# Starting the mixture of experts inside cross attention, with the token weights moved into the up product

## The chip, the cores and the metric

One core of one Trainium2 chip runs the whole program. The metric is the device time of one execution in microseconds. TensorE (PE, with its weight loads shown apart as PEld), VectorE (DVE), ScalarE (ACT), GpSimd (POOL) and SyncE (SP, which only issues DMAs here) each run an instruction queue in order and wait for each other by semaphores.

## What is computed

A decoder block on 16 batches of 56 tokens with 128 features, in float32:

```python
x = x + self_attn(layernorm(x))                  # token and channel diffusion
x = x + cross_attn(layernorm(x), ctx)            # ctx: 16 x 1500 x 128, 16 heads of depth 8
x = x + moe(layernorm(x))
# moe: E, I, K = 8, 512, 2
logits = x_flat @ gate_w.T                       # 896 tokens x 8 experts
top_v, top_i = top_k(logits, 2); probs = softmax(top_v)
combine = sum of probs * one_hot(top_i)          # weight of each token for each expert
for each expert e:
    hidden = silu(x_flat @ wg[e].T) * (x_flat @ wu[e].T)
    out += combine[e][:, None] * (hidden @ wd[e].T)
```

Every expert is computed for every token; the weight is zero for six of the eight.

## The kernel before

The kernel has three stages. The first is self attention. The second is cross attention, one batch after another in a software pipeline (`pipelined`, bodies for batch 0, a loop over pairs, and the last three batches unrolled). A batch has 12 slots `t`, one for each 125 keys: in each TensorE makes the scores (L1307), ScalarE their exponentials (L1103), and at slots 0, 5 and 9 TensorE weighs values (L1323) for four slots at once. Score banks are used in turn, so scores of slot t wait for the exponential of t-2. Between them the projections and maxima of the next batches are placed. At slot 8 the output projection of the batch before stands (L1339), and VectorE adds it to `X` (L1195). `X` holds two batches (a pair) side by side, 56 rows from partition 0 and 56 from partition 64, eight pairs.

After the last weighing come the denominators (L1332), their inverse (L1185), the output product and the residual of batch 15. Then the block ends: all engines meet, and a second block holds the experts. There VectorE takes the statistics of all eight pairs (L128, L133), GpSimd the power -1/2 (L156, L159), VectorE normalises (L138), TensorE transposes (L1646), ScalarE copies the transposed tokens twice, once rounded (`T_hi`) and once in full (`T3`, L1533), and VectorE subtracts them (`T_lo`, L1560). SyncE moves `X` by 23 small DMAs into `X3`, 7 tiles of 128 tokens without gaps.

A matmul on rounded operands (fp32r) takes one pass; a plain float32 one appears as two instructions. Gate and up products are therefore split: hi x hi, hi x lo, lo x hi, three passes of 448 columns (half of the tokens), where the weights are rounded by ScalarE (L1525) and their remainder is taken by GpSimd (L1506). An expert has 8 units: 2 halves of tokens x 4 tiles of 128 hidden features. In each unit TensorE makes gate (L1684 to L1686, banks 0 and 1) and up (the same lines, banks 2 and 3), ScalarE the SiLU (L1541), VectorE the product with up (`hidden`, L1629). The down products of the expert before stand between the units, plain float32, with the hidden tile as the still operand and `w_down` moving, four t of 128 x 128 for each of the 7 token tiles (L1664). VectorE multiplies each tile's result by the tokens' weight and adds it to `X3` (L1618). The routing (L1569 to L1604) runs on VectorE between the first expert's products; its exponential (L1545) stands on ScalarE between SiLUs. The result leaves in one DMA (L1497). Weights are loaded with two buffers; the first two experts' loads stand on SP behind cross attention's last batch.

The two calls of the units' order are, on TensorE:

```python
for side, done in ((0, gate_done), (1, up_done)): ...three passes...      # L1680
if later(e, 1) and k < TT:
    down(e - 1, 1 - j, k)                                                # L1688
```

## Time and profile before

| | us |
|---|---|
| median of 3 runs | 646.02 (645.42 to 651.07) |
| profiled execution, whole | 653.12 |
| its span, first to last instruction | 651.3 |
| cross attention's last weighing ends, in the span | 496.39 |
| first gate product starts | 515.55 |
| last down product ends | 647.52 |

In the rows that follow, a time is microseconds from the span's start. Shapes are partitions x elements, "x448" is the number of instructions. "Busy" of a group is the time in which at least one of them runs: matmuls overlap, so the mean duration of one is longer than the distance from one to the next. The granted clock of TensorE is given as a share of 2.4 GHz; 0.50 is 1.2 GHz.

### The profile page before, as it was taken

The page shows a single profiled execution, that of the slowest core. Times are in us where ns is not written, and L with a number is a line of the kernel's source. Part 1 is how long each engine was busy: PE and PEld are TensorE (multiplying, and loading weights), DVE is VectorE, ACT ScalarE, POOL GpSimd, SP SyncE. Part 2 cuts the span into 40 slices and gives each one's busy share as a digit, 9 for nine tenths or more (in the row PEclk, how much of TensorE's full clock was granted, in tenths as well). Part 3 has the DMA queues.
Part 4 walks back from the last instruction along what each step waited for, and adds up shares of the span by engine and source line. Part 5 has one row for each costly group of instructions (what it writes and reads, how often), then busy time and mean ns, then how long its engine had stood idle before and what let it go on. Part 6 is the DMA issues. An engine that isn't in the chain of part 4 may idle for free. (4 is left out here: it accounts for less than half of the span.)

```text
span 651.3 us, 17561 instructions
## 1 busy us (share of the span) xinstructions
PE 593.1 (91%) x6732; PEld 481.7 (74%) x6732; DVE 427.2 (66%) x799; ACT 338.2 (52%) x506; POOL 183.2 (28%) x149
## 2 busy tenths in 40 slices
PE   3799787798999999999999999999985699999997
PEld 1566374376877877877877787787774589999997
DVE  4765357866887788778788788877822464444443
ACT  2466445274666576567566566657564353333321
POOL 4685305622223323224223232322100221111100
PEclk9789789798999999999999999999998599999999
DMA  5000006498267356446536736734620011111100
GB/s 211 1 3 3 0 3 133 94 193 192 68 132 183 96 140 144 119 117 142 144 92 141 172 88 127 179 100 91 144 100 1 17 46 49 48 48 48 48 17 29
DMA packets 26190, 60.29 MB, mean 93 GB/s; under 512 B 14368, under 2 KB 15392, under 8 KB 26152
## 3 DMA queue, kind: packets, MB, share of 16 engines
q1 hardware_dynamic: 26152, 59.77, 38.3%
q8 instruction: 26, 0.43, 0.3%
q14 instruction: 12, 0.10, 0.0%
HBM read 20.48 MB, written 0.46 MB: 32 GB/s over the span
## 5 line engine op out<-in xcount | busy, mean ns | idle before, releaser
L1163 DVE TENSOR_REDUCE chunk_max<-PS 128x1 f32<-128x500 f32 x336 | 214.3, 673 | 62.2 <-PE PS L1283 60.5
L1103 ACT ACTIVATE P<-PS 125x896 f32<-125x896 f32 x192 | 173.3, 913 | 124.1 <-PE PS L1307 123.4
L1283 PE MATMUL PS<-k_hi,q_block_hi 128*128 128x500 f32 x336 | 131.3, 438 | 6.5 <-ACT k_full L246 3.3
L1307 PE MATMUL PS<-q_stack,k_stack 97*125 97x224 f32 x768 | 122.5, 283 | 4.3 <-DMA q_stack<-neg_rows 2.4
L1307 PEld LDWEIGHTS PS<-q_stack,k_stack 97*125 97x125 f32 x768 | 106.9, 190 | 19.3 <-issue 8.9
L255 POOL TENSOR_TENSOR k_lo<-k_full,k_hi 128x500 fp32r<-128x500 f32 x48 | 61.1, 1276 | 104.7 <-ACT k_full L246 102.4
L1283 PEld LDWEIGHTS PS<-k_hi,q_block_hi 128*128 128x128 f32 x336 | 60.9, 193 | 37.1 <-ACT k_full L246 16.7
L1629 DVE TENSOR_TENSOR hidden<-gated,PS 128x448 f32<-128x448 f32 x64 | 39.6, 619 | 69.2 <-PE PS L1686 63.8
L1323 PE MATMUL PS<-P,values 125*32 125x112 f32 x3072 | 84.4, 262 | 0.6 <-ACT P L1103 0.5
L1323 PEld LDWEIGHTS PS<-P,values 125*32 125x32 f32 x3072 | 72.6, 110 | 14.3 <-issue 10.8
L1541 ACT ACTIVATE gated<-PS 128x448 f32<-128x448 f32 x64 | 34.8, 544 | 80.5 <-PE PS L1686 76.0
L1036 POOL TENSOR_TENSOR q_stack<-q_copies,consts 96x896 fp32r<-96x896 f32 x16 | 26.8, 1677 | 132.1 <-PE PS L1307 131.6
L1664 PEld LDWEIGHTS PS<-w_down,hidden 128*128 128x128 f32 x448 | 57.6, 191 | 1.5
L1664 PE MATMUL PS<-w_down,hidden 128*128 128x128 f32 x448 | 57.9, 274 | 0.0
L217 PE MATMUL PS<-ctxT,mats 128*128 128x500 f32 x96 | 50.2, 607 | 4.3 <-ACT k_full L246 2.7
L1684 PE MATMUL PS<-T_hi,w_hi 128*128 128x448 f32 x128 | 52.2, 408 | 1.5 <-DVE hidden L1629 1.5
L225 PE MATMUL PS<-mats,ctxT 128*125 128x128 f32 x384 | 49.9, 273 | 0.0
L225 PEld LDWEIGHTS PS<-mats,ctxT 128*125 128x125 f32 x384 | 48.0, 188 | 1.4 <-issue 0.2
L1686 PE MATMUL PS<-T_hi,w_lo 128*128 128x448 f32 x128 | 47.4, 371 | 0.0
L1685 PE MATMUL PS<-T_lo,w_hi 128*128 128x448 f32 x128 | 47.3, 370 | 0.0
L245 ACT ACTIVATE k_hi<-PS,cols 128x500 fp32r<-128x500 f32 x48 | 32.2, 670 | 24.1 <-PE PS L217 23.4
L1506 POOL TENSOR_TENSOR w_lo<-w_gate_up,w_hi 128x1024 fp32r<-128x1024 f32 x8 | 19.0, 2380 | 91.1 <-ACT w_hi L1525 91.1
(153 smaller groups left out, 666.7 us busy)
## 6 DMA issues: line engine op xcount, KB each, us to landing
k_stack<-k_hi SPq DMA_DIRECT2D x128, 187.5 KB, 4.5
ctxT<-ctx_in SPq DMA_DIRECT2D x16, 750.0 KB, 4.3
k_stack<-k_lo SPq DMA_DIRECT2D x64, 187.5 KB, 4.4
w_gate_up<-wgu_in SPq DMA_DIRECT2D x8, 512.0 KB, 3.7
w_down<-wd_in SPq DMA_DIRECT2D x8, 256.0 KB, 2.7
q_stack<-neg_rows SPq DMA_DIRECT2D x112, 0.5 KB
mats<-mats_in SPq DMA_DIRECT2D x1, 832.0 KB, 5.2
q_copies<-q_hi SPq DMA_DIRECT2D x8, 98.0 KB, 4.4
```

What stands on the lines that cost most here:

```text
L217: nc.tensor.matmul(bank[:, 0:KW], MAT["wk"], ctxT[:, j, KW * c:KW * c + KW], start=True, stop=True).then_inc(k_projected, 1)
L225: last = nc.tensor.matmul(bank[0:KR, 128 * t:128 * t + 128], ctxT[:, j, k0:k0 + KR], MAT["wv"], start=True, stop=True)
L255: nc.gpsimd.tensor_tensor(k_lo[:, j, k], k_full[:, k], k_hi[:, j, k].bitcast(F32), ALU.subtract).then_inc(k_lo_ready, 1)
L1103: nc.scalar.activation(P[:, t % RING, :].rearrange("p (a n) -> p a n", a=2), PS[0:KR, 2 * (t % 2):2 * (t % 2) + 2, 0:HALF], ACT.Exp).then_ ...
L1163: nc.vector.tensor_reduce(out=chunk_max[:, n // KC, n % KC:n % KC + 1], in_=PS[:, max_bank(b, n), 0:KW], axis=AX.X, op=ALU.max).then_inc(m ...
L1283: nc.tensor.matmul(PS[:, max_bank(b, n), 0:KW], q_block_hi[:, j, 128 * t:128 * t + 128], k_hi[:, j, KW * c:KW * c + KW], start=True, stop= ...
L1307: last = nc.tensor.matmul(PS[0:KR, 2 * (t % 2) + g // 2, o:o + GH * N], k_stack[:, j, g, KR * t:KR * t + KR], q_stack[0:SHIFT_ROW + 1, j, ...
L1323: last = nc.tensor.matmul(PS[32 * k:32 * k + 32, 6, 2 * N * r:2 * N * r + 2 * N], values[:, j, t, g, :], P[:, t % RING, 2 * N * g:2 * N * ...
L1664: last = nc.tensor.matmul(PS[:, 4 + 2 * j + p // 4, 128 * (p % 4):128 * (p % 4) + 128], hidden[:, j, t, 128 * p:128 * p + 128], w_down[:, ...
L1684: nc.tensor.matmul(bank, w_hi[:, j, w], hi, start=True, stop=False)
L1685: nc.tensor.matmul(bank, w_hi[:, j, w], lo, start=False, stop=False)
L1686: nc.tensor.matmul(bank, w_lo[:, j, w], hi, start=False, stop=True).then_inc(done, 1)
```

## The change

The second block is gone; the experts stand in the block of cross attention.

In batch 13 SyncE loads both first experts' weights. In batch 14 ScalarE rounds expert 0's gate and up weights at slots 4 and 6, and VectorE takes at slot 8 the statistics of the seven finished pairs (14 of 16 batches), waits for GpSimd's power and normalises them. In batch 15 TensorE transposes them at slot 1 (two groups: pairs 0 to 3, and 4 to 6), makes the logits of the first 448 tokens at slot 4, turns their weights at slot 9 and spreads them at slot 11; VectorE copies and splits the transposed tokens (slots 0 and 8), routes the first half (slot 5), copies the turned weights (slot 10) and weighs the tokens for expert 0 (slot 11); ScalarE has the exponential of the routing at slot 6 and a rounding at slot 8. After the last weighing TensorE begins with the first expert's gates for the first 448 tokens, and the last pair (batches 14 and 15) is normalised, transposed and routed between products of experts 0 and 1. The tokens stand with the pairs' pitch, so that the 23 moves fall away.

The weight of a token for an expert is multiplied into the token before the up product: the up operand is `w * T`. For each expert the weight row is picked and spread over 128 partitions by one product per half (`pick_now`, 448 columns, rounded operands), VectorE multiplies it by `T3` (`weigh_tokens`), ScalarE rounds and GpSimd subtracts. Gate products stand one expert ahead of up products and their SiLUs are kept (`gated`, 8 units, two buffers).

Per unit: VectorE multiplies the SiLU into up's bank in PSUM (`multiply`), ScalarE rounds it to SBUF (`round_hidden`), VectorE takes the remainder (`split_hidden`), and TensorE makes three passes with the down weights still and the hidden values moving, 448 columns (`down`), three units later. All experts' down products are summed in two PSUM banks (6 and 7). Up and spread share banks 2 to 5 in turn. `w_down` is rounded by ScalarE and split by GpSimd. At the end ScalarE copies each half of the sums, TensorE turns it batch by batch with plain float32 products of 128 columns (`turn_out`), VectorE adds it to `X`, and two DMAs store it.

The core of the diff, with indentation shortened (not shown: buffers and semaphores, the helpers `norm_stats`, `norm_pairs`, `copy_turned`, `turn_group`, `route_logits`, `turn_weights` and `route`, whose VectorE steps are those of before on 4 pairs each, ending with a rounded copy and a remainder, and the removed block):

```diff
+def gate_turn(e, k):
+    if isinstance(e, int) and e < 2:
+        return IT * (2 * (k // IT) + e) + k % IT
+    return UNITS * e + k
+def use_bank(j, use):
+    return PS[:, 2 + (len(UP_USES) * j + UP_USES.index(use)) % 4, 0:HALF]
+def spread_bank(e, j, c):
+    if isinstance(e, int) and e == 0:
+        return PS[:, SPREAD_BANKS[c], 0:HALF]
+    return use_bank(1 - j, ("spread", c))
+def use_released(e, use):
+    kind, n = use
+    return (hidden_split, UNITS * e + n + 1) if kind == "up" else (xw_ready, 2 * (e + 1) + n + 1)
...
+            if isinstance(b, int) and b == B - 3:
+                for e in range(2):
+                    load_gate_up(sp, e, e)
+                    load_down(sp, e, e)
         pipelined(sp, period, B)
...
+        def load_expert(e, j, u):
+            if exists(e + 2, E):
+                sp.wait_ge(down_split, e + 1)
+                load_gate_up(sp, e + 2, j)
+                load_down(sp, e + 2, j)
+        load_expert(0, 0, 0)
+        other_experts(sp, load_expert)
+        for c in range(2):
+            sp.wait_ge(summed, c + 1)
+            sp.dma_start(out[:, HP * c:HP * c + HP, :], X[:, HP * c:HP * c + HP, :]).then_inc(stored, 16)
...
+        split_gate_up(0, 0, 1, up_rounded, up_split)
+        layernorm_power(pool, 5, slice(0, PAIRS - 1))
+        split_weighted(0, 0, 0)
+        split_gate_up(1, 1, 0, gate_rounded, gate_split)
+        split_down(0, 0)
+        layernorm_power(pool, 6, slice(PAIRS - 1, PAIRS))
+        split_weighted(0, 0, 1)
+        pool.wait_ge(y3_turned, 3)
+        nc.gpsimd.memset(outT[:, :, N:PITCH], 0.0).then_inc(out_cleared, 1)
+        def expert(e, j, u):
+            if exists(e + 1, E):
+                split_gate_up(e + 1, 1 - j, 1, up_rounded, up_split)
+                split_weighted(e + 1, 1 - j, 0)
+                split_down(e + 1, 1 - j)
+            if exists(e + 2, E):
+                split_gate_up(e + 2, j, 0, gate_rounded, gate_split)
+            if exists(e + 1, E):
+                split_weighted(e + 1, 1 - j, 1)
+        expert(0, 0, 0)
...
         def period(b, j, u):
             for t in range(KT):
                 exps(b, t)
+                if isinstance(b, int) and b == B - 2 and t in (4, 6):
+                    side = (4, 6).index(t)
+                    round_gate_up(0, 0, 0, side, (gate_rounded, up_rounded)[side])
+                if isinstance(b, int) and b == B - 1:
+                    if t == 6:
+                        exp_weights(0)
+                    if t == 8:
...
+        round_weighted(0, 0, 0)
         copy_sums(B - 1)
+        silu(0, 0, 0)
+        round_down(0, 0, 0)
+        for k in range(1, IT):
+            silu(0, 0, k)
+        silu(1, 1, 0)
+        round_hidden(0, 0, 0)
+        silu(1, 1, 1)
+        silu(1, 1, 2)
+        round_hidden(0, 0, 1)
+        silu(1, 1, 3)
+        exp_weights(1)
+        for k in range(IT, UNITS):
+            silu(0, 0, k)
+        for k in range(IT, UNITS):
+            silu(1, 1, k)
+            if k == IT + 1:
+                act.wait_ge(weights_turned, 2)
+                nc.scalar.copy(weight_rows[:, 1, :], PS[0:2 * E, ROWS_BANKS[1], 0:HALF]).then_inc(rows_copied, 1)
+        round_hidden(0, 0, 2)
+        round_weighted(0, 0, 1)
+        round_hidden(0, 0, 3)
+        round_gate_up(1, 1, 0, 1, up_rounded)
+        round_weighted(1, 1, 0)
+        round_hidden(0, 0, 4)
+        round_down(1, 1, 0)
+        round_hidden(0, 0, 5)
+        round_gate_up(2, 0, 1, 0, gate_rounded)
...
+        def expert(e, j, u):
+            for k in range(UNITS):
+                if exists(e + 1, E):
+                    silu(e + 1, 1 - j, k)
+                round_hidden(e, j, k)
+                if exists(e + 1, E):
+                    if k == 0:
+                        round_gate_up(e + 1, 1 - j, u if j == 0 else u + 1, 1, up_rounded)
+                    if k == 3:
+                        round_weighted(e + 1, 1 - j, 0)
+                    if k == 4:
+                        act.wait_ge(down_done, UNITS * e)
+                        round_down(e + 1, 1 - j, u if j == 0 else u + 1)
+                    if k == 7:
+                        round_weighted(e + 1, 1 - j, 1)
+                if k == 5 and exists(e + 2, E):
+                    round_gate_up(e + 2, j, u + 1, 0, gate_rounded)
+        other_experts(act, expert)
+        act.wait_ge(out_cleared, 1)
+        for c in range(2):
+            act.wait_ge(down_done, UNITS * (E - 1) + IT * (c + 1))
+            nc.scalar.copy(outT[:, B // 2 * c:B // 2 * c + B // 2, 0:N],
+                           PS[:, 6 + c, 0:HALF].rearrange("p (b n) -> p b n", n=N)).then_inc(out_copied, 1)
...
+        def weigh_tokens(e, j, c):
+            if later(e, 1):
+                dve.wait_ge(xw_split, 2 * (e - 1) + c + 1)
+            dve.wait_ge(spread, 2 * e + c + 1)
+            nc.vector.tensor_tensor(xw[c], spread_bank(e, j, c), T3[:, c * HALF:(c + 1) * HALF], ALU.mult
+                                    ).then_inc(xw_ready, 1)
+        def last_period(t):
+            if t == 0:
+                copy_turned(0)
+                for e in range(2):
+                    pick(e, e)
+            if t == 5:
+                route(0)
+            if t == 8:
+                copy_turned(1)
+            if t == 10:
+                dve.wait_ge(weights_turned, 1)
+                nc.vector.tensor_copy(weight_rows[:, 0, :], PS[0:2 * E, ROWS_BANKS[0], 0:HALF]).then_inc(rows_copied, 1)
+            if t == 11:
+                weigh_tokens(0, 0, 0)
...
+        def multiply(e, j, k):
+            dve.wait_ge(gated_ready, gate_turn(e, k) + 1)
+            dve.wait_ge(up_done, UNITS * e + k + 1)
+            bank_ = use_bank(j, ("up", k))
+            nc.vector.tensor_tensor(bank_, gated[:, j, k, :], bank_, ALU.mult).then_inc(hidden_ready, 1)
+        def split_hidden(e, j, k):
+            dve.wait_ge(hidden_rounded, UNITS * e + k + 1)
+            nc.vector.tensor_tensor(hid_lo[:, k % RING3, :], use_bank(j, ("up", k)), hid_hi[:, k % RING3, :].bitcast(F32),
+                                    ALU.subtract).then_inc(hidden_split, 1)
...
+        norm_stats(range(PAIRS - 1, PAIRS))
+        multiply(0, 0, 0)
+        dve.wait_ge(rstd_ready, 7)
+        norm_pairs(2)
+        split_hidden(0, 0, 0)
+        copy_turned(2)
+        multiply(0, 0, 1)
+        route(1)
+        split_hidden(0, 0, 1)
+        multiply(0, 0, 2)
+        weigh_tokens(0, 0, 1)
+        split_hidden(0, 0, 2)
+        multiply(0, 0, 3)
+        split_hidden(0, 0, 3)
+        weigh_tokens(1, 1, 0)
+        for k in range(IT, UNITS):
+            multiply(0, 0, k)
+            if k > IT:
+                split_hidden(0, 0, k - 1)
+            if k == 5:
+                weigh_tokens(1, 1, 1)
+            if k == 6:
+                pick(2, 0)
+        def expert(e, j, u):
+            for k in range(UNITS):
+                multiply(e, j, k)
+                if k >= 1:
+                    split_hidden(e, j, k - 1)
+                else:
+                    split_hidden(e - 1, 1 - j, UNITS - 1)
+                if exists(e + 1, E) and k in (2, 5):
+                    weigh_tokens(e + 1, 1 - j, (2, 5).index(k))
+                if k == 6 and exists(e + 2, E):
+                    pick(e + 2, j)
+        other_experts(dve, expert)
+        split_hidden(E - 1, 1, UNITS - 1)
+        for c in range(2):
+            dve.wait_ge(out_turned, c + 1)
+            part = X[:, HP * c:HP * c + HP, :]
+            nc.vector.tensor_tensor(part, part, PS[:, c, :].rearrange("p (a d) -> p a d", d=D), ALU.add
+                                    ).then_inc(summed, 1)
...
+        def last_period(t):
+            if t == 1:
+                turn_group(0)
+                turn_group(1)
+            if t == 4:
+                route_logits(0)
+            if t == 9:
+                turn_weights(0)
+            if t == 11:
+                spread_weights(0, 0, 0)
...
+        def three_passes(bank_, hi, lo, moving_hi, moving_lo, start=True, stop=True, **more):
+            nc.tensor.matmul(bank_, hi, moving_hi, start=start, stop=False, **more)
+            nc.tensor.matmul(bank_, hi, moving_lo, start=False, stop=False, **more)
+            return nc.tensor.matmul(bank_, lo, moving_hi, start=False, stop=stop, **more)
+        def gates(e, j, k):
+            c, t = k // IT, k % IT
+            turn = gate_turn(e, k)
+            if k == 0:
+                pe.wait_ge(gate_split, e + 1)
+            if isinstance(e, int) and e == 0:
+                pe.wait_ge(t_split, (1, 3)[c])
+            if later(turn, 2):
+                pe.wait_ge(gated_ready, turn - 1)
+            w = slice(128 * t, 128 * t + 128)
+            three_passes(PS[:, k % 2, 0:HALF], w_hi[j][0][:, w], w_lo[j][0][:, w], T_hi[:, c, :], T_lo[:, c, :]
+                         ).then_inc(gate_done, 1)
...
+        def up(e, j, k):
+            c, t = k // IT, k % IT
+            if k == 0:
+                pe.wait_ge(up_split, e + 1)
+            if t == 0:
+                pe.wait_ge(xw_split, 2 * e + c + 1)
+            take_use(e, ("up", k))
+            w = slice(128 * t, 128 * t + 128)
+            three_passes(use_bank(j, ("up", k)), w_hi[j][1][:, w], w_lo[j][1][:, w], xw_hi[j][c], xw_lo[j][c]
+                         ).then_inc(up_done, 1)
+        def down(e, j, k, first=False, final=False):
+            c, t = k // IT, k % IT
+            if k == 0:
+                pe.wait_ge(down_split, e + 1)
+            pe.wait_ge(hidden_split, UNITS * e + k + 1)
+            three_passes(PS[:, 6 + c, 0:HALF], d_hi[:, j, t, :], d_lo[:, j, t, :], hid_hi[:, k % RING3, :], hid_lo[:, k % RING3, :],
+                         first and t == 0, final and t == IT - 1, skip_group_check=True).then_inc(down_done, 1)
         for w in range(QUAD):
             weigh(B - 1, 1, KT - QUAD + w)
+        gates(0, 0, 0)
         denominators(B - 1)
+        for k in range(1, IT):
+            gates(0, 0, k)
         project_out(B - 1, 1)
...
+                spread_next(0, 0, 1)
+            if k == UNITS - 2:
+                down(0, 0, IT, True)
+        def expert(e, j, u):
+            stop = isinstance(e, int) and e == E - 1
             for k in range(UNITS):
-                act.wait_ge(gate_done, UNITS * e + k + 1)
-                if later(e, 1) or k >= 2:
-                    act.wait_ge(hidden_ready, UNITS * e + k - 1)
-                nc.scalar.activation(gated[:, k % 2, :], PS[:, k % 2, 0:HALF], ACT.Silu
-                                     ).then_inc(gated_ready, 1)
-                if k == 3 and isinstance(e, int) and e == 0:
-                    act.wait_ge(route_shifted, 1)
-                    nc.scalar.activation(weight[:, :, :], weight[:, :, :], ACT.Exp).then_inc(route_exp, 1)
-                if k == 1 and (not isinstance(e, int) or e + 1 < E):
-                    round_weights(e + 1, 1 - j, u if j == 0 else u + 1)
-        experts(act, period)
...
+                        spread_next(e, j, (2, 5).index(k))
+                    gates(e + 1, 1 - j, k)
+                up(e, j, k)
+        other_experts(pe, expert)
+        def turn_out(c):
+            pe.wait_ge(out_copied, c + 1)
+            if c == 0:
+                pe.wait_ge(gated_ready, UNITS * E)
+            for b in range(8 * c, 8 * c + 8):
+                p = b // 2 % 4
+                last = nc.tensor.matmul(PS[PITCH * (b % 2):PITCH * (b % 2) + PITCH, c, 128 * p:128 * p + 128],
+                                        outT[:, b, :], C["ident"], start=True, stop=True)
+            last.then_inc(out_turned, 1)
+        for k in range(UNITS - LAG, UNITS):
+            down(E - 1, 1, k, False, True)
+            if k == UNITS - LAG:
+                turn_out(0)
+        turn_out(1)
```

## Rows read from the trace of the kernel before

**Rows 1.** The page's first and second part: TensorE's busy time and clock.

```profile
PE 593.1 (91%) x6732; PEld 481.7 (74%) x6732; DVE 427.2 (66%) x799; ACT 338.2 (52%) x506; POOL 183.2 (28%) x149
PEclk9789789798999999999999999999998599999999
```

**Rows 2.** Busy time by stretch; the first line names the columns.

```profile
core 0: us, PE busy (x) PEld busy (x) DVE busy (x) ACT busy (x) POOL busy (x), PEclk, DMA share, GB/s
160.00:490.00 330.00, 323.40 (x4304) 260.72 (x4302) 255.66 (x408) 208.58 (x293) 90.72 (x64) 1.00 0.54 125
502.00:515.00 13.00, 4.60 (x20) 3.89 (x20) 7.37 (x26) 4.07 (x6) 4.17 (x3) 0.50 0.03 9
545.00:560.00 15.00, 15.00 (x100) 14.36 (x99) 6.63 (x16) 5.29 (x9) 2.38 (x1) 1.00 0.15 54
```

**Rows 3.** Chain that ended last, in order of time: start, us, what.

```profile
546.88 0.89 PE PS L1664 x8
548.99 0.89 PE PS L1664 x8
...
562.82 0.89 PE PS L1664 x8
```

**Rows 4.** Timeline of the seam: start, us, engine, line, operation, count.

```profile
494.35 2.04 PE L1323 MATMUL PS<-P,values 125*32 125x112 f32 x64
499.59 1.53 PE L1339 MATMUL PS<-mats,heads_out 128*56 128x128 f32 x8 [2.09 <-DVE heads_out L1189]
501.16 0.29 DVE L1195 TENSOR_TENSOR X<-X,PS 56x128 f32<-56x128 f32 x1 [1.62 <-PE PS L1339]
501.78 1.64 DVE L128 BATCH_NORM_STATS2 stats<-X 128x6 f32<-128x128 f32 x8 [0.33 <-PEq L951]
504.47 1.66 POOL L159 TENSOR_TENSOR rstd<-rstd,minus_half 128x8 f32<-128x8 f32 x1
506.10 2.34 POOL L1506 TENSOR_TENSOR w_lo<-w_gate_up,w_hi 128x1024 fp32r<-128x1024 f32 x1
506.17 4.15 DVE L138 TENSOR_SCALAR Y<-X,moments,rstd 128x128 f32<-128x128 f32 x8 [2.07 <-POOL rstd L159]
```

**Rows 5.** The same timeline where the experts begin.

```profile
515.55 0.72 PE L1684 MATMUL PS<-T_hi,w_hi 128*128 128x448 f32 x1
516.82 0.57 PE L1684 MATMUL PS<-T_hi,w_hi 128*128 128x448 f32 x1
517.93 0.57 PE L1684 MATMUL PS<-T_hi,w_hi 128*128 128x448 f32 x1
520.85 2.39 POOL L1506 TENSOR_TENSOR w_lo<-w_gate_up,w_hi 128x1024 fp32r<-128x1024 f32 x1 [12.41 <-ACT w_hi L1525]
521.02 2.30 DVE L1579 TENSOR_TENSOR weight<-logit,best 128x56 f32<-128x56 f32 x1
522.93 1.28 ACT L1545 ACT_TABLE_LOAD   x1
524.49 1.28 ACT L1541 ACT_TABLE_LOAD   x1
```

**Rows 6.** Groups by line, 480 to 652 us: busy us, mean ns | idle before.

```profile
L1629 DVE TENSOR_TENSOR hidden<-gated,PS 128x448 f32<-128x448 f32 x64 | 39.6, 619 | 69.2 <-PE PS L1686 63.8 <-ACT gated L1541 4.9
L1541 ACT ACTIVATE gated<-PS 128x448 f32<-128x448 f32 x64 | 34.8, 544 | 80.5 <-PE PS L1686 76.0 <-DVE hidden L1629 4.5
L1506 POOL TENSOR_TENSOR w_lo<-w_gate_up,w_hi 128x1024 fp32r<-128x1024 f32 x8 | 19.0, 2380 | 91.1 <-ACT w_hi L1525 91.1
L1525 ACT CAST w_hi<-w_gate_up 128x1024 fp32r<-128x1024 f32 x8 | 8.3, 1042 | 7.6 <-PEq L951 5.0 <-DMA w_gate_up<-wgu_in 2.5
```

**Rows 7.** Timeline of the last batch of cross attention.

```profile
481.33 0.95 PEld L1307 LDWEIGHTS PS<-q_stack,k_stack 97*125 97x125 f32 x8 [0.17 <-issue]
482.07 0.92 ACT L1103 ACTIVATE P<-PS 125x896 f32<-125x896 f32 x1 [1.38 <-PE PS L1307]
483.96 1.57 DVE L1185 RECIPROCAL heads_out<-PS 128x112 f32<-128x112 f32 x2 [8.65 <-PE PS L1332]
```

**Rows 8.** Timeline of the end.

```profile
641.11 6.41 PE L1664 MATMUL PS<-w_down,hidden 128*128 128x128 f32 x56
648.45 0.35 SPq L1497 DMA_DIRECT2D out<-X  x1
```

506 lines of the change are left out of this document (265 added, 241 removed).

## Prediction

> **What bounds the kernel now.** I read the page's first part, then the busy time by stage, then the groups of the last 170 us by line, then the chain, then the timeline at the seams. TensorE is the busiest engine [rows 1]. By stage [rows 2] it is busy 98% of cross attention's middle and 100% of the experts' stage, with a granted clock of 1.00 in both. Between them it starves: in 502 to 515 us it is busy 4.6 of 13 us at clock 0.50. So the experts cost what TensorE's stream costs, and the seam costs a serial chain.
>
> The stream: the chain runs through TensorE alone. A down tile stands at 546.88 and the same tile of the next expert at 562.82 [rows 3], so an expert is 15.94 us. A group of eight down products takes 0.89 us there and follows the last at 2.10, which leaves 1.21 for six products of 448 columns (gate and up of one unit in three passes each): 0.2017 us per pass. Check: 48 x 0.2017 + 7 x 0.89 = 15.9.
>
> The seam [rows 4]: the last weighing ends at 496.39. Then heads' sums, inverse, output product (499.59), residual (501.16), statistics of all pairs (501.78), power on GpSimd (504.47, 1.66), eight normalised pairs (4.15, the first of which waits behind GpSimd's split), transposes, copies, logits; the first gate product starts at 515.55 [rows 5]. That is 19.2 us from the weighing's end. It then runs at 0.37 per pass (three passes from 516.82 to 517.93), until the clock is back at about 520.5.
>
> **The change: the steady part.** Removed: 7 tiles x 0.89 = 6.2 us of down products per expert, and the weighted adds. Added: 8 units x 3 passes of down with 448 columns, and two spreading products of 448 columns (rounded operands, so one pass each): 26 passes. A new expert is 48 + 26 = 74 passes x 0.2017 = 14.93 us, 1.0 less than now. All passes have the shape and type of those measured, so I take the same price.
>
> What must hide under 1.87 us per unit: VectorE multiplies and splits every unit, 2 x 0.62 [rows 6], and weighs tokens twice per expert: 8 x 1.24 + 2 x 0.62 + a pick of 0.2 = 11.4 of 14.9 us. ScalarE: 16 instructions of 448 at 0.54, two more for tokens, and 1536 columns of weights at 1.04 per 1024 [rows 6]: 9.8 + 1.6 = 11.4 us. GpSimd: 1536 columns of weights and 896 of tokens at 2.38 per 1024: 5.7 us. No engine is near TensorE. The order holds too: a split stands behind the next unit's multiply, so it ends about 1.87 + 0.7 + 0.62 = 3.2 us after its up product; down comes three units later (5.6 us minus the unit's own products), and the bank is wanted again after four uses (over 3.7 us). VectorE writing into PSUM has no row here: below, the 0.62 of reading it; above, twice that, since each element would go through twice. At 1.24 VectorE needs 16.4 us per expert and would bound. I take 0.62.
>
> **A rule against it.** In the rows, a VectorE subtraction of 56 columns from SBUF took 2.30 us because GpSimd's split stood from 520.85 to 523.24 [rows 5], while the products with a PSUM operand keep a mean of 0.62 over all 64 [rows 6]. The Trainium skill (SBUF — State Buffer, Who interferes with whom) says that a VectorE instruction with two SBUF inputs is shut out by a GpSimd one that reads SBUF, and one with at most one SBUF input is not. The trace agrees in both cases; the new steady instructions have one SBUF input each.
>
> **Cross attention's last two batches.** ScalarE rounds two halves of weights in batch 14 (0.55 each, in places with 0.6 us of slack and one with none): +0.3 us. Statistics and seven normalised pairs sit in VectorE's idle 8.65 us before 483.96 [rows 7]: 2.1 + 1.9 for the power + 7 x 0.27 = 5.9 us (0.27 from the pairs after GpSimd's split ended at 508.44: 1.88 / 7 [rows 4]), ready near 481.2, before TensorE asks at 481.9. In the last batch TensorE gains 7 transposes (14 passes x 0.111, from 0.89 for eight: 1.6 us), 4 logit products (0.9), 4 turned weights (0.9), one spread (0.2). The period is not bound by either engine but by their alternation: ScalarE idles 1.38 us during each weighing, TensorE idles up to 0.8 us elsewhere. Walking through the slots, the transposes cost 1.5 us, the logits nothing more, the turned weights 0.9. Sum +2.4, with batch 14 +2.7. Both ends for the range: 0 if it all fills gaps, 4.5 (3.6 of products, 0.9 of ScalarE's) if none does.
>
> **The new seam**, from the last weighing's end to the loop over later experts. TensorE's work: 29 groups of three passes (16 gates, 8 ups, 5 downs) x 0.605 = 17.5; three spreads 0.6; denominators and output 1.5; one transpose, logits and turned weights 2.0. Together 21.6 us. Its waits, in order: the first SiLU needs a table load of 1.28 [rows 5] and a rounding stands behind it, 1.4 in all; the last pair's normalisation behind residual, statistics and power, 0.9; the exponential of the second half of the routing is between two table loads, and gate 6 of the first expert waits for the SiLU after it, 1.8; after the route's dozen VectorE steps (about 4.6 us, 0.2 to 0.47 each) the splits of units 2 and 3 stand behind the token weighing, 1.3 + 1.3; down 4 waits 0.9; refilling the pipeline 0.8. That is 8.4, so 30.0 us. The clock: the weighing leaves it at 1.00, and no wait here is over 1.8 us, against about 7 us of nearly idle TensorE in which it fell before. So I price all at full rate; at half rate a group costs 3 x 0.17 = 0.5 more, which for half of the groups is +7 us: the upper end.
>
> The table loads have a rule as well. In the rows they stand 1.56 us apart with the 0.25 us exponential between them and the SiLU right behind, 1.28 each [rows 5]. The Trainium skill (ScalarE: Activation LUTs, What ACT_TABLE_LOAD costs) adds a drain of 1.38 us to each switch; for the exponential's two switches that would be +2.8 us, 641 for the profiled sum below. The trace shows no such gap.
>
> **The sum**, in the profiled execution's time. Last weighing 496.4 + 2.7 = 499.1. Seam 30.0: 529.1. Then until the last up product: 8 x 24 groups less 29 and less the last 3 downs = 160 x 0.605 = 96.8, 12 spreads 2.4, and 0.5 because the last expert has no gates and VectorE's 1.24 per unit just exceeds 1.21: 628.8. Tail after the last up product: multiply, round, split 2.0; meanwhile turning half the output; two downs 1.2 behind it; copy 0.7, turning eight batches (16 x 0.111 and waiting 1.2), an add of 512 columns 0.7, store 2.85 as now. In order that comes to 9.6 us, against 10.0 now (641.27 to 651.3) [rows 8]. End: 638.4, which is 12.9 under the span of 651.3. The profiled execution took 653.1 in all and the median of the runs is 646.0; taking the difference over, 646.0 - 12.9 = 633.
>
> The barrier between the blocks, the 23 moves by DMA and the wait for code on ScalarE go away with it; they are within the 19.2 us, not counted again. The weight loads move to batch 13, ahead of key stack loads that have over 12 us to spare.
>
> **Rivals.** (a) The forecast: 633, chance 0.52; own range 629 to 637. (b) The seam stays serial, or the clock falls in it: new code sits on four engines in hand-written order, so one late step stalls all. For: the route and table chain. Against: no single long wait found. +7: 640, chance 0.22. (c) Insertions hide and seam waits overlap: 2.7 + 2 less: 628, chance 0.12. (d) VectorE is locked by GpSimd in the steady part. GpSimd holds 5.7 us per expert; if each of its instructions delayed VectorE fully, VectorE needs 11.4 + 5.7 = 17.1, 2.2 over TensorE's 14.9, for seven experts +15.4, and +4 for the route in the seam: 652.5, slower. It decides from 16.8 us per expert of VectorE. Against: 0.62 throughout [rows 6]. Writing PSUM at the upper price gives 16.4, 7 x 1.5 = +10, 643.5. Chance for both 0.10, 0.04 of it slower by over 1%. (e) The early start doesn't take place: gates wait inside the last period for normalised pairs or split weights, so the chain moves into cross attention and holds back its exponentials. +6: 639, chance 0.04.
>
> One per cent is 6.5 us, about what a measurement can tell. Below 639.6 lie (a), (c) and half of (b) and (e): faster 0.78. Within 1%: 0.16. Slower: 0.06. The range of 8 in 10 runs from 626 to 642.
>
> **What would show it.** In the new profile: experts 14.9 us apart; passes 0.20 apart; VectorE at about 76% of the steady part with instructions of 0.62; the last weighing 2 to 3 us later; TensorE busy some 70% of the 30 us after it with clock near 1.00; under 10 us from last up product to end. Wrong if a unit takes over 1.95 us, if the granted clock is 0.50 for long after the weighing, or if multiplies take over 0.7 us.

## The result, and the profile after

| | before | after |
|---|---|---|
| median of 7 runs, us | 647.83 (645.42 to 651.07) | 640.74 (636.57 to 642.47) |
| ratio, with its 95% interval | | 0.9894 (0.9853 to 0.9935) |
| profiled execution: span, us | 651.3 | 634.6 |
| its clock over the whole span | 0.960 | 0.989 |

An eighth execution of the kernel after, outside this median, took 645.76 us. The change makes the kernel 1.1% faster, 7.1 us by the medians, and between 4.2 and 9.5 by the interval. The time is inside the range of the prediction, and the gain is about half of the 12.9 us forecast.

The two spans cannot be subtracted. The page's first and second part after:

```profile
PE 586.0 (92%) x6542; PEld 462.8 (73%) x6542; DVE 460.2 (73%) x849; ACT 380.5 (60%) x602; POOL 214.4 (34%) x184
PEclk9999999699999999999999999999999999999999
```

Beside [rows 1] the clock's row shows two things. The 5 near the end, the half-rate seam, is gone; that is the change. But the 7s and 8s of the first ten slices are gone too, but for one 6, and there both kernels do the same work: this one execution simply had a better clock in self attention. So I measure from a mark behind that stage which the change cannot move, the last stacking of queries. On GpSimd's timeline it stands before at 458.03 us and after at

```profile
449.95 1.68 POOL L1159 TENSOR_TENSOR q_stack<-q_copies,consts 96x896 fp32r<-96x896 f32 x1 [9.34 <-PE PS L1714]
```

Already there the two executions are 8.1 us apart. From the mark to the end is 193.3 us before and 184.65 after: 8.7 less, which fits the runs. All kernels below are read in this way, one profiled execution each. The columns: mark to end; mark to the end of the last weighing; from there to the sixth down product of the experts ("seam"); from that to the start of the last up pass ("loop"); from that to the end ("tail"). The forecast's row is its own sum: 638.4 - 458.0 = 180.4, 499.1 - 458.0 = 41.1, then 30.0, 99.7 and 9.6.

| kernel | mark to end | to weighing | seam | loop | tail |
|---|---|---|---|---|---|
| before | 193.3 | 38.4 | | | |
| forecast | 180.4 | 41.1 | 30.0 | 99.7 | 9.6 |
| after | 184.7 | 39.1 | 29.8 | 106.1 | 9.6 |
| after, another execution | 185.6 | 40.1 | 29.8 | 106.1 | 9.6 |

Seam and tail are as forecast, the weighing comes 1 to 2 us sooner than forecast, and the loop takes 6.4 us more. That one stage holds the whole error, and more: the earlier weighing hides a part of it.

**Steady part of after.** Busy time by stretch, columns as in [rows 2]: two stretches of the seam, and one of the loop.

```profile
500.00:504.00 4.00, 2.33 (x13) 1.83 (x11) 3.41 (x13) 3.94 (x6) 0.00 (x0) 1.00 0.00 0
516.00:520.00 4.00, 3.19 (x15) 2.29 (x14) 3.88 (x8) 2.77 (x7) 3.62 (x4) 1.00 0.20 53
560.00:600.00 40.00, 40.00 (x189) 34.75 (x189) 26.36 (x49) 27.21 (x56) 16.06 (x13) 1.00 0.12 40
```

In the loop TensorE is busy 40.00 of 40 us at clock 1.00. By that row alone nothing is lost, since matmuls overlap, and a short gap at the front of one lies under the end of the one before (below, the product at 561.13 lasts 0.47 us and the next starts at 561.53). The weight loads tell more: 34.75 us of 40, where [rows 2] had 14.36 of 15 before, with another mix of products. Something may hold the loads up. TensorE's timeline after (start, us of one) shows where:

```profile
560.63 0.36 PE L1859 MATMUL PS<-hid_lo,d_hi 128*128 128x448 f32 x1
560.83 0.37 PE L1860 MATMUL PS<-hid_hi,d_lo 128*128 128x448 f32 x1
561.13 0.47 PE L1798 MATMUL PS<-weight_rows,pick_now 16*128 16x448 f32 x1
561.53 0.47 PE L1858 MATMUL PS<-T_hi,k_hi 128*128 128x448 f32 x1
561.84 0.37 PE L1859 MATMUL PS<-T_lo,k_hi 128*128 128x448 f32 x1
562.04 0.37 PE L1860 MATMUL PS<-T_hi,k_lo 128*128 128x448 f32 x1
```

Passes follow each other at 0.20 to 0.21. The spreading product L1798 is the only one with 16 rows of contraction. It starts 0.30 after the pass before it, the next pass starts 0.40 after it, and the one after that 0.31 later: 1.01 us for three distances that would be 0.61 at 0.20 each, so 0.4 more than I had given it.

**The seam of after**, same timeline, with ScalarE's rows:

```profile
496.86 0.45 PE L1858 MATMUL PS<-T_hi,k_hi 128*128 128x448 f32 x1
...
500.44 1.28 ACT L1283 ACT_TABLE_LOAD   x1
501.73 0.23 ACT L1283 ACTIVATE weight<-weight 112x32 f32<-112x32 f32 x1
501.98 1.28 ACT L1316 ACT_TABLE_LOAD   x1
503.27 0.98 ACT L1316 ACTIVATE gated<-PS 128x448 f32<-128x448 f32 x2
503.96 0.44 PE L1858 MATMUL PS<-T_hi,k_hi 128*128 128x448 f32 x1 [1.67 <-ACT gated L1316]
```

Gates and ups now stand where TensorE starved before, and the granted clock stays at 1.00, against 0.50 in 502 to 515 us of [rows 2]. TensorE's longest wait in the seam is the 1.67 us behind the table loads (forecast 1.8).

**VectorE and ScalarE** after, groups by line, 480 to 636 us:

```profile
L1582 DVE TENSOR_TENSOR PS<-gated,PS 128x448 f32<-128x448 f32 x64 | 40.2, 628 | 35.7 <-PE PS L1860 34.2
L1586 DVE TENSOR_TENSOR hid_lo<-PS,hid_hi 128x448 fp32r<-128x448 f32 x64 | 39.6, 618 | 1.0 <-ACT hid_hi L1322 0.9
```

The multiply that writes into PSUM takes 628 ns, the split that writes into SBUF 618: the lower bound of the price was right.

### The profile page after: what moved, and what is told of

Same layout as the page of the kernel before. It is cut to its first block, busy times and chain, and to the rows that moved or that the text cites. A ratio compares the mean times of both kernels' runs of the same rounds, so it can differ in the third digit from the quotient of the medians.

```text
span 634.6 us, 17321 instructions
## 1 busy us (share of the span) xinstructions
PE 586.0 (92%) x6542; PEld 462.8 (73%) x6542; DVE 460.2 (73%) x849; ACT 380.5 (60%) x602; POOL 214.4 (34%) x184
## 3 DMA queue, kind: packets, MB, share of 16 engines
q1 hardware_dynamic: 25104, 59.38, 39.3%
## 4 chain that ended last, share of the span: by engine, by line
PE 70%; DVE 5%; SPq 4%; ACT 3%; issue 2%; DMA 1%; ACTq 0%; POOL 0%; DVEq 0%
PE PS L1730 12%; PE PS L1714 12%; PE PS L1690 11%; PE PS L1858 6%; PE PS L225 6%; PE PS L1860 6%; PE PS L1859 5%; PE PS L217 5%; PE PS L1746 3%; DVE chunk_max L1417 2%; ACT k_full L246 1%; SPq L1079 1%; SPq L1072 1%; PE PS L1798 1%; SPq L1087 1%
## 5 line engine op out<-in xcount | busy, mean ns | idle before, releaser
L255 POOL TENSOR_TENSOR k_lo<-k_full,k_hi 128x500 fp32r<-128x500 f32 x48 | 61.1, 1277 | 102.4 <-ACT k_full L246 100.2
L1582 DVE TENSOR_TENSOR PS<-gated,PS 128x448 f32<-128x448 f32 x64 | 40.2, 628 | 35.7 <-PE PS L1860 34.2
L1322 ACT CAST hid_hi<-PS 128x448 fp32r<-128x448 f32 x64 | 34.1, 533 | 39.1 <-DVE PS L1582 39.1
L217 PE MATMUL PS<-ctxT,mats 128*128 128x500 f32 x96 | 48.4, 587 | 4.3 <-ACT k_full L246 2.7
L1586 DVE TENSOR_TENSOR hid_lo<-PS,hid_hi 128x448 fp32r<-128x448 f32 x64 | 39.6, 618 | 1.0 <-ACT hid_hi L1322 0.9
L263 DVE TENSOR_TENSOR values<-PS,rows 125x512 f32<-125x512 f32 x48 | 33.1, 691 | 4.7 <-PE PS L225 3.6
L246 ACT ACTIVATE k_full<-PS,cols 128x500 f32<-128x500 f32 x48 | 31.9, 665 | 0.0
L1192 POOL TENSOR_TENSOR k_lo<-w_gate_up,k_hi 128x512 fp32r<-128x512 f32 x16 | 20.6, 1285 | 23.4 <-ACT k_hi L1278 23.4
L1858 PE MATMUL PS<-T_hi,k_hi 128*128 128x448 f32 x64 | 25.6, 400 | 2.4 <-ACT gated L1316 2.3
```

Of the source, the lines that this page charges most:

```text
L217: nc.tensor.matmul(bank[:, 0:KW], MAT["wk"], ctxT[:, j, KW * c:KW * c + KW], start=True, stop=True).then_inc(k_projected, 1)
L246: nc.scalar.activation(k_full[:, k], bank[:, 0:KW], ACT.Identity, bias=COL["bk"]).then_inc(k_ready, 1)
L255: nc.gpsimd.tensor_tensor(k_lo[:, j, k], k_full[:, k], k_hi[:, j, k].bitcast(F32), ALU.subtract).then_inc(k_lo_ready, 1)
L1582: nc.vector.tensor_tensor(bank_, gated[:, j, k, :], bank_, ALU.mult).then_inc(hidden_ready, 1)
L1586: nc.vector.tensor_tensor(hid_lo[:, k % RING3, :], use_bank(j, ("up", k)), hid_hi[:, k % RING3, :].bitcast(F32), ALU.subtract).then_inc(hi ...
L1858: nc.tensor.matmul(bank_, hi, moving_hi, start=start, stop=False, **more)
```

## The experiments

Two theories stood for the slower loop. **Shape (S):** changing from 128 rows of contraction to 16 and back costs TensorE about 0.4 us. **Waits (W):** semaphore waits or bank releases around the spread hold TensorE up, whatever its shape. A further question was whether anything else than TensorE's stream bounds the loop (P says the stream does), and what carries the gain at all: the clock kept up by the early start (C), or the shorter chain of the work.

### Spread with 128 rows

```diff
- weight_rows = sb3("weight_rows", [2 * E, 2, HALF], F32R)
- pick_now = sb3("pick_now", [2 * E, 2, D], F32R)
+ weight_rows = sb3("weight_rows", [128, 2, HALF], F32R)   # rows 16.. zeroed once by GpSimd
+ pick_now = sb3("pick_now", [128, 2, D], F32R)            # rows 16.. hold whatever the constant has
```

The rows that are added multiply zeros (not shown: the zeroing, and the copies into rows 0 to 15). TensorE's waits, the banks and their order stay; VectorE and ScalarE wait once more, for the zeroing in batch 14.

> The changed kernel with both operands of the spreading product taken from 16 to 128 partitions (rows 16 to 127 of the weights are zero). Theory S (shape): the 0.40 us that a spreading product costs beyond its own pass come from switching between 16 and 128 rows. It expects 0.20 to 0.21 us from pass to pass through the spread, experts 15.0 to 15.1 us apart instead of 15.85, and an end 5 to 6 us earlier from the same point of cross attention on. Theory W (waits): the time goes to the semaphore waits in front of the spread. It expects experts still 15.8 us apart and no gain. The extra memset on GpSimd lies in its idle time in batch 14.

TensorE's timeline:

```profile
542.47 0.37 PE L1864 MATMUL PS<-hid_hi,d_lo 128*128 128x448 f32 x1
542.68 0.36 PE L1802 MATMUL PS<-weight_rows,pick_now 128*128 128x448 f32 x1
542.88 0.36 PE L1862 MATMUL PS<-T_hi,k_hi 128*128 128x448 f32 x1
```

Its busy time by stretch:

```profile
560.00:600.00 40.00, 40.00 (x199) 37.06 (x198) 28.61 (x53) 28.00 (x57) 16.21 (x13) 1.00 0.12 40
```

The product with eight times the rows is cheaper: the distances are 0.21 and 0.20, and the same 40 us hold 199 matmuls instead of 189, both at 40.00 busy. Ratio to before 0.9810 (0.9775 to 0.9846), median 636.36 against 648.74. S holds and W falls, since every wait of TensorE is still there.

### The kernel after once more, as the neighbour of these runs

> The changed kernel once more beside the padded one, on the same chip: 0.985 to 0.994 of the kernel before by either theory, spreads 0.6 us of TensorE's time each.

No edit. Median of 12 runs 642.73, ratio 0.9913 (0.9888 to 0.9939), which does not overlap with that of the padded kernel. Its profiled execution gives the same seam and loop as the first, within 0.01 us; only the stretch up to the weighing differs, by 0.9.

### Spread with 64 rows

The same edit with 64 in place of 128.

> The spreading product on 64 partitions. Theory S with a switch at any other row count than the neighbours' 128: still 0.6 us per spread, experts 15.85 us apart. If the loss grows with the distance from 128 rows, something between 0.2 and 0.6. Theory W: 0.6.

```profile
542.99 0.37 PE L1864 MATMUL PS<-hid_hi,d_lo 128*128 128x448 f32 x1
543.28 0.47 PE L1802 MATMUL PS<-weight_rows,pick_now 64*128 64x448 f32 x1
543.69 0.47 PE L1862 MATMUL PS<-T_hi,k_hi 128*128 128x448 f32 x1
```

Nothing is gained: 0.29 us before the product and 0.41 after it, loop 106.1. So the price does not grow with the rows that are missing; 16 and 64 cost the same, 128 nothing.

### The spread twice

```diff
+ for again in range(2):
      nc.tensor.matmul(spread_bank(e, j, c), pick_now[:, j, :], weight_rows[:, c, :], ...)
```

> The changed kernel with each spreading product issued twice, the same operands into the same bank, and no wait between the two. Theory S: the second has the rows of the first, so it adds one plain pass, 0.19 to 0.21 us, 16 times: +3.2 us. A theory that a product of 16 rows costs 0.6 us by itself expects +0.6 each, +9.6 us. Theory W expects 0.2 each as S does.

```profile
532.85 0.67 PE L1799 MATMUL PS<-weight_rows,pick_now 16*128 16x448 f32 x2
533.44 0.47 PE L1860 MATMUL PS<-T_hi,k_hi 128*128 128x448 f32 x1
```

One row holds both. The next pass follows the first of them at 0.59, where a single spread has 0.40: the second costs 0.20, as any pass. So it is the change of shape that costs, once for the pair, not the product. In the loop that gives 12 x 0.20 = 2.4, measured 2.3. The seam grew by 2.6 where three products explain 0.6. In the rest of it the clock was low: granted 0.56 in 514 to 518 us and 0.59 in 518 to 522 (more on this under the table of all kernels).

### Less work in the stream

This kernel leaves out one of the three down passes (hidden's rounded part times the remainder of the down weights), 8 passes per expert, and keeps all else.

```diff
- three_passes(..., d_hi, d_lo, hid_hi, hid_lo, ...)
+ nc.tensor.matmul(bank_, d_hi[:, j, t, :], hid_hi[:, k % RING3, :], start=start, stop=False, ...)
+ nc.tensor.matmul(bank_, d_hi[:, j, t, :], hid_lo[:, k % RING3, :], start=False, stop=stop, ...)
```

> The changed kernel with two down passes in place of three: the product of the rounded hidden values with the remainder of the down weights is left out, so down is less exact. Theory P (TensorE's stream bounds the experts' part): 56 passes fewer in experts 0 to 6, 0.2033 each, make 11.4 us, and up to 1.6 in the last expert where TensorE waits already: 11 to 13 us less than the changed kernel, experts about 14.2 us apart. Theory R (the round trip multiply, round, split bounds, since VectorE and ScalarE now work two thirds of the time): under 6 us, with TensorE waiting for hid_lo in each unit.

Measured: median 630.26, ratio 0.9710 (0.9676 to 0.9744). Experts stand 14.17 us apart (543.35 to 557.52), 1.65 less than after's 15.82; 8 x 0.2 is 1.6. The loop is 10.8 us shorter. TensorE's stream bounds, as P says; VectorE and ScalarE, which have the same work in less time, are not reached. Its seam came out 1.6 us longer although five passes fewer stand in it. The edit does not explain that, but the clock does: it was granted 0.55 in 518 to 522 us and 0.59 in 522 to 526, and up to 518.14 this seam had been 0.2 us ahead of the kernel after's.

### The early start held back

The second, third and fourth tile's gates of the first expert, and with them the four groups that follow, are issued behind the last output product and the last transpose: seven groups of three passes, 4.2 us. VectorE takes the last pair first. Nothing is added or left out; TensorE only has nothing to do while it waits.

```diff
  gates(0, 0, 0)
  denominators(B - 1)
+ project_out(B - 1, 1)
+ turn_group(2)
  for k in range(1, IT):
      gates(0, 0, k)
- project_out(B - 1, 1)
...
+ norm_pairs(2); copy_turned(2)      # VectorE: before multiply(0, 0, 0), not after
```

> The changed kernel with three of the first gates and everything of experts 0 and 1 behind them held back until the last pair is normalised and turned; VectorE normalises and copies that pair before its first product. Nothing is left out. Theory H (what the early start gives is only the time it covers): the 4.2 us of seven groups no longer lie in the wait, +3.5 to +4.5 us against the changed kernel, clock at 1.00 throughout. Theory C (the early start also keeps the clock up): TensorE has under 3 us of work in the 8 us after the last weighing, its granted clock falls to 0.50 as it did in the kernel before, and the first groups take 1.1 us each: +7 to +9 us.

Busy time by stretch:

```profile
498.00:502.00 4.00, 1.21 (x8) 0.83 (x8) 1.74 (x5) 0.56 (x2) 2.20 (x3) 0.73 0.19 58
502.00:506.00 4.00, 3.50 (x10) 2.91 (x11) 1.08 (x4) 1.09 (x2) 0.06 (x1) 0.50 0.39 138
506.00:510.00 4.00, 4.00 (x19) 3.71 (x19) 1.52 (x3) 2.42 (x5) 0.00 (x0) 0.91 0.00 0
...
526.00:530.00 4.00, 3.80 (x11) 2.43 (x10) 2.77 (x6) 2.59 (x5) 2.43 (x2) 0.65 0.00 0
```

TensorE's timeline in the second stretch:

```profile
503.52 0.57 PE L1860 MATMUL PS<-T_hi,k_lo 128*128 128x448 f32 x1
503.89 0.57 PE L1858 MATMUL PS<-T_hi,k_hi 128*128 128x448 f32 x1
...
506.80 0.37 PE L1860 MATMUL PS<-T_hi,k_lo 128*128 128x448 f32 x1
```

TensorE is busy 1.21 of 4 us, the clock falls to 0.50, and passes stand 0.37 apart until about 506.5. The seam is 35.6 instead of 29.8, the whole 6.7 to 7.6 us longer than after's; 1.0 to 2.0 of that lie ahead of the weighing's end, where the edit changes nothing. Median 648.1, ratio 0.9993 (0.9974 to 1.0012): the gain is gone, although the new down products, the route in PSUM and the missing barrier are all still in. Without the early start the rest of the change gains nothing that the runs can tell. The seam's 5.8 us lie between the two expectations. The fall of the clock is C's, and H's clock at 1.00 is refuted, but in the gates it explains only 1.9 us (ten distances from 502.63 to 506.51 take 3.9 us and would take 2.0). A second fall, in 526 to 530 us, adds 0.6: up to it this seam was 5.1 behind the kernel after's, at its end 5.7. What remains, some 3.2 us, is time in which TensorE has nothing at hand: its two long waits there, for the heads' sums and for the last pair, are 2.09 and 2.23 us. How much of these the clock lengthened, no run tells apart.

### The table loads taken out

The exponential of the second half of the routing is replaced by a SiLU, so that its two table loads fall away; the routing weights of those tokens are then another function's.

```diff
- nc.scalar.activation(own, own, ACT.Exp)
+ nc.scalar.activation(own, own, ACT.Silu if c else ACT.Exp)
```

> The changed kernel with the second half's routing exponential computed as a SiLU, so that ScalarE needs no change of tables there (the routing weights of the second half are wrong numbers, the work is the same). The 1.67 us that TensorE waits for the SiLU behind the two table loads should go: -1.6 us if nothing else is late there; 0 to -0.5 if VectorE's routing chain, which runs until then, is the next to be waited for.

The seam is 28.3 instead of 29.8, loop and tail unchanged. The wait of 1.67 us at 503.96 is gone with its cause, and 1.5 us with it. Median 640.06, ratio 0.9880 (0.9845 to 0.9915): next to the kernel after's 0.9913 (0.9888 to 0.9939) the runs do not tell 1.5 us. The trace does: its clock stayed at 1.00 through the seam, and three seams of the unchanged spread at that clock agree within 0.05 us. It is one execution all the same.

### The last expert: three attempts

With the padded spread the loop takes 101.3 us. The forecast has 99.7. 0.8 of the difference is that a unit of nine passes takes 1.83 and not 1.815 us (160/3 units). The rest is in the last expert, which has no gates, so that a unit of TensorE is only 1.21. VectorE's timeline of the padded kernel:

```profile
614.38 0.62 DVE L1590 TENSOR_TENSOR hid_lo<-PS,hid_hi 128x448 fp32r<-128x448 f32 x1
615.05 0.63 DVE L1586 TENSOR_TENSOR PS<-gated,PS 128x448 f32<-128x448 f32 x1
...
616.63 0.63 DVE L1586 TENSOR_TENSOR PS<-gated,PS 128x448 f32<-128x448 f32 x1 [0.43 <-PE PS L1864]
617.17 0.61 DVE L1590 TENSOR_TENSOR hid_lo<-PS,hid_hi 128x448 fp32r<-128x448 f32 x1
```

Two units take 2.8 us (splits at 614.38 and 617.17), 1.40 each, and every second multiply waits for TensorE. The forecast had 1.24, VectorE's own work, as if it never waited. What closes the loop: a bank that comes free too late, the order on VectorE, or the order on TensorE? First the bank: the last expert's ups take their banks in a ring of their own.

```diff
+ if e == E - 1 and k >= 2:
+     pe.wait_ge(hidden_split, UNITS * e + k - 3)    # released by the split four units back
```

> The kernel with the padded spreading product, and in the last expert the up products take all four of their banks in turn instead of leaving the two turns of the spreading products empty (an up product then waits for the split of the unit four before it, not three). If the bank's return sets the last expert's pace (theory B), its ups come down from 1.40 us apart to about 1.25 and the time from the sixth down product to the last up falls by 1 to 1.4 us. If it is the order of multiply and split on VectorE with the wait for the hidden remainder in front of down (theory D), nothing changes, within 0.2 us.

Loop 101.32 us, as without it (101.31). It is not the banks. Its neighbour in the same comparison was the padded kernel again:

> The padded kernel once more on the same chip as the one beside it: 0.978 to 0.985 of the kernel before, 179.8 us from the last stacking of queries to the end in its profiled execution, give or take 0.5.

Median 636.78, ratio 0.9828 (0.9786 to 0.9870), beside 0.9779 (0.9736 to 0.9823) for the ring; the intervals overlap and the stretches are alike but for the seam's clock (below), so I take the two as equal. The second measurement of the padded kernel agrees with the first.

Then VectorE's order, the split of a unit ahead of the next multiply:

```diff
- multiply(e, j, k); split_hidden(e, j, k - 1)
+ split_hidden(e, j, k - 1); multiply(e, j, k)       # last expert only
```

> The kernel with the padded spreading product, and in the last expert VectorE's split of a unit ahead of the next unit's multiply. There the up products stand 1.43 us apart instead of the 1.22 of six passes, and TensorE waits for hid_lo every second unit. If the order on VectorE is the cause, the last expert gets 1 to 1.5 us shorter than in the padded kernel; if the round trip over three engines is, nothing changes or it gets longer by up to 1 us. Against the kernel before: 0.979 or 0.981.

TensorE's timeline, in the last expert and in the tail:

```profile
619.32 0.47 PE L1866 MATMUL PS<-hid_hi,d_hi 128*128 128x448 f32 x1 [0.28 <-DVE hid_lo L1590]
621.09 0.47 PE L1866 MATMUL PS<-hid_hi,d_hi 128*128 128x448 f32 x1 [0.29 <-DVE hid_lo L1590]
...
627.90 1.98 PE L1968 MATMUL PS<-consts,outT 128*64 128x128 f32 x16 [2.40 <-ACT outT L1382]
```

Worse: a unit takes 1.77, because the split waits for ScalarE's rounding of the product just made and the next multiply now stands behind it. Loop 102.4, and the tail 12.8 instead of 9.6. Median 638.9, ratio 0.9864 (0.9838 to 0.9891); the runs alone would not tell it from the padded kernel's 0.9828. The tail shows the clock a second time:

```profile
624.00:628.00 4.00, 1.31 (x7) 0.59 (x7) 2.80 (x5) 1.50 (x3) 0.00 (x0) 0.94 0.00 0
628.00:632.00 4.00, 3.79 (x22) 2.98 (x22) 0.76 (x2) 0.17 (x1) 0.00 (x0) 0.63 0.13 50
```

After 1.31 busy of 4 us the granted clock is 0.63, and the turning product takes 1.98 us, against 1.09 in after.

Last TensorE's order: in the last expert the down products follow four units behind, not three.

```diff
+ if stop and k >= LAG:                  # last expert
+     if k > LAG:
+         down(e, j, k - LAG - 1, False, stop)
```

> The kernel with the padded spreading product, and in the last expert the down products four units behind the up products instead of three. Theory L (a loop of order: split of unit k-3, its down, up k, multiply k, and then the split of unit k-1, 2.8 us for two units, sets the last expert's 1.4 us per unit; in the swapped version the loop was round and split between two multiplies, 1.77 us per unit, as measured): with four units of distance the loop spreads over three units, the ups come 1.21 to 1.27 us apart as in a pure stream, the last up product comes 1 to 1.3 us earlier and the tail gains nothing, since its extra down fills a wait of 1.15 us there: -1 us in all, 0.98 of the kernel before. If the loop is another, no change.

VectorE's timeline:

```profile
617.46 0.62 DVE L1586 TENSOR_TENSOR PS<-gated,PS 128x448 f32<-128x448 f32 x1
618.65 0.63 DVE L1586 TENSOR_TENSOR PS<-gated,PS 128x448 f32<-128x448 f32 x1
619.86 0.63 DVE L1586 TENSOR_TENSOR PS<-gated,PS 128x448 f32<-128x448 f32 x1
621.07 0.63 DVE L1586 TENSOR_TENSOR PS<-gated,PS 128x448 f32<-128x448 f32 x1
```

Multiplies now stand 1.2 apart without a wait, and the loop takes 100.0. So the loop of 2.8 us was up, multiply, round, split, down, next up: a down product that waits for its split holds the next up behind it in TensorE's queue. It gives 1.3 us; the median of 636.73, ratio 0.9830 (0.9804 to 0.9856), does not resolve that beside the padded kernel's 0.9828.

All in the table's columns:

| kernel | mark to end | to weighing | seam | loop | tail |
|---|---|---|---|---|---|
| spread 128 rows | 179.8 | 39.4 | 29.4 | 101.3 | 9.6 |
| the same again | 180.5 | 39.1 | 30.5 | 101.3 | 9.6 |
| with ring | 179.7 | 39.3 | 29.5 | 101.3 | 9.6 |
| with swap | 184.8 | 39.0 | 30.6 | 102.4 | 12.8 |
| with lag of four | 179.3 | 40.3 | 29.5 | 100.0 | 9.6 |
| spread 64 rows | 185.0 | 39.4 | 29.9 | 106.1 | 9.6 |
| spread twice | 189.7 | 39.4 | 32.4 | 108.4 | 9.6 |
| one down pass less | 175.1 | 39.2 | 31.5 | 95.3 | 9.2 |
| held back | 192.2 | 41.1 | 35.6 | 106.0 | 9.6 |
| table loads out | 183.1 | 39.2 | 28.3 | 106.1 | 9.6 |

**The clock in the seam.** The seams fall into two sorts. Where the granted clock stayed at 1.00 they repeat: 29.82 to 29.87 us with the spread on 16 or 64 rows (three executions), 29.44 to 29.47 with it on 128 (three). Where the clock fell they are longer: the padded kernel's second execution, the swap, the doubled spread, the left-out pass and the held one. Of the padded kernel's second execution, the clock's row of its page (the 8 near the end is 508 to 524 us) and two rows of TensorE's timeline:

```profile
PEclk9889899899999999999999999999999989999999
518.09 0.58 PE L1862 MATMUL PS<-k_hi 128*128 128x448 f32 x1
518.46 0.58 PE L1863 MATMUL PS<-k_lo,k_hi 128*128 128x448 f32 x1
```

Up to 24 us behind the weighing its passes stand where those of the first execution stand, within 0.02 us. Then they follow each other at 0.37, and the sixth down product comes 1.1 us later. Nothing in the kernel differs. TensorE had been busy 2.20 of the 4 us from 514 to 518, in the first execution 2.22, where the clock stayed. So the early start keeps the clock up in some executions and not in all; how often it falls in those that were only timed, no run tells.

The padded spread, alone, with the ring or with the lag of four, is the best version that computes everything: 1.7 to 2.2% faster than before in four comparisons whose intervals overlap, against 0.9 to 1.1% for the change itself.

## Why the prediction was right and wrong

**The step that failed: two spreads at the price of a pass.** "26 passes ... All passes have the shape and type of those measured, so I take the same price." They do not: the spread has 16 rows. It costs 0.61 us, not 0.20. With two per expert that is 14.93 + 0.82 = 15.75, measured 15.8 (545.33, 561.13, 576.97), where the padded kernel shows 15.06 (542.68, 557.74). The steady part was to gain 1.0 us per expert and gained 0.1. For the loop: 12 x 0.41 = 4.9 of its 6.4 us. The rule of the prediction, to bound from both sides what the trace does not show, was applied to VectorE's writes and not to this product, whose shape stands nowhere in the trace of before. The padded kernel confirms the price: its loop is 4.8 us shorter. A bound was there to be read: in [rows 7] the weight loads of the scores, 97 x 125, begin after 0.17 us in which TensorE waited for nothing that the profile shows, and the products before them, the weighing's, have weights of 32 columns. That is a change of another kind than from 128 rows to 16, but it is the nearest row, and it has a price. At 0.17 each way and 16 spreads the sum would have been 5.4 us longer.

The Trainium skill (TensorEngine Tiling (Array Packing), Key Properties) states that a change of the tiling mode drains TensorE. If a product on fewer rows counts as such a change, which the page does not say, the traces agree in kind: two spreads in a row cost one such stop each way, and 64 rows as much as 16. The Trainium skill (TensorE: Matmul & The Clock Gate, LDWEIGHTS) says that a weight load goes by its columns, not by its rows; the load itself does, 0.18 us here with 16 rows and 0.19 with 128. The price lies in the gaps around it.

**Passes.** A unit of nine took 1.83 against 1.815: +0.8 in the loop. **Last expert.** 1.40 per unit and not 1.24: +1.1. Both engines' own work was counted, but not the round between them. VectorE's own work was even taken too high: it was busy 26.36 of 40 us in the loop, 66% and not 76%, because an instruction can start before the one ahead of it ends (the split at 617.17 stands 0.54 behind a multiply of 0.63). Together 99.7 + 4.9 + 0.8 + 1.1 = 106.5; measured 106.1.

**Cross attention's last batches.** +0.8 and +1.7 measured, 2.7 forecast: inside the bounds of 0 and 4.5. The other kernels of the table have the same work there and take 39.0 to 41.1, so +0.6 to +2.7: the forecast is the upper end of what happens. This hid 1 to 2 us of the miss.

**The seam.** 30.0 forecast, 29.8 measured in both executions. The sum is right, its terms less so, and that is partly luck. Counted as in the forecast, from start to start less 0.20, the waits are about 6.6 us and not 8.4: the first SiLU 1.2 (forecast 1.4), the last pair none (0.9; the transpose at 496.78 follows the pass at 496.58 without a wait), the table loads 2.2 with the pass that follows late (1.8), the two splits 0.8 and 1.2 (1.3 each), the fifth down 1.0 (0.9), refilling 0.3 (0.8). Against that the three spreads cost 0.4 each. Little of this reaches the end: with the padded spread the seam is 0.4 us shorter, not 1.2, since TensorE then waits 0.90 instead of 0.50 for the split in front of the third down. The table loads' wait was worth 1.5 by experiment.

The clock stayed at 1.00 in both executions, but the reason given for it does not hold. The prediction sets its short waits "against about 7 us of nearly idle TensorE in which it fell before". Busy time by stretch, before:

```profile
498.00:500.00 2.00, 0.41 (x4) 0.41 (x5) 1.50 (x3) 0.00 (x0) 0.00 (x0) 1.00 0.00 0
500.00:502.00 2.00, 1.12 (x7) 0.70 (x4) 0.51 (x3) 0.19 (x1) 0.00 (x0) 0.52 0.00 0
```

It fell at about 500 us, 3.7 behind the weighing's end, with heads' sums and a part of the output product in between; the 7 idle us come after. So the margin was thinner than priced, and in several of the other executions it was gone. The held kernel is what the rival (b), +7 us, looks like when it happens: 6.7 to 7.6 us, of which the seam has 5.8.

One reading of the prediction has no row: "the wait for code on ScalarE". Its 5.01 us ahead of the rounding at 501.81 end with the barrier between the blocks. No term rests on it.

**Tail.** 9.6 and 9.56. The two turning products and the pair of downs between them, TensorE's timeline after:

```profile
627.20 1.09 PE L1960 MATMUL PS<-consts,outT 128*64 128x128 f32 x16 [1.15 <-ACT outT L1379]
...
630.33 1.09 PE L1960 MATMUL PS<-consts,outT 128*64 128x128 f32 x16 [0.62 <-ACT outT L1379]
```

**VectorE and GpSimd.** Neither part of rival (d) took place: 628 and 618 ns with GpSimd busy 16 of 40 us beside them. This agrees with the rule cited in the prediction from the Trainium skill (SBUF — State Buffer, Who interferes with whom) for instructions with one SBUF input.

**Table loads.** The drain that the rule would add is not in this trace either: load, 0.23 us exponential, load and SiLU follow each other at 1.29, 0.25 and 1.29.

**The number.** The mechanism was right: TensorE's stream bounds the experts, and the early start covers the serial chain. For the change as made the sum of 180.4 from the mark was 4 to 5 us short; the spread alone makes 4.9. The padded kernel comes out at the sum (179.8, 180.5), partly by luck: its weighing is 1.7 to 2.1 us sooner and its loop 1.6 longer than forecast. The 640 that was measured is what rival (b) gives, but not by its mechanism.

## What to carry to other kernels

Check each added matmul's rows of contraction against its neighbours in the stream. One product on 16 or 64 rows between 128-row ones cost 0.4 us more here; filling it up with zero rows takes that away, and a second such product beside the first costs only its own 0.20. In a loop that shows TensorE as 100% busy, look at the weight loads' busy share and at the distance from start to start: only these showed the loss. When work is to be begun early, what counts is that TensorE has it at hand while the serial chain runs; moving seven groups behind the chain gave back the whole gain. And before a stretch's microsecond is explained, look at its granted clock: here two executions of one kernel differ by 1.1 us in one stretch for that reason alone.
